# Tokens normalized inside the second graph layer, expert tiles gathered by an inverse list and scattered in token order

## What is computed

```python
x = x + gcn(_layernorm(x), edges, edge_weight)          # 2 graph layers, each segment_sum over 50000 edges
# _L0_ffn_ref on xt = _layernorm(x):
logits = xt @ Wr + br
probs = softmax(logits); top_p, top_idx = top_k(probs, 2)
weights = top_p / top_p.sum(-1)
xn = (xt - mu) * rsqrt(var + 1e-5)                      # a second normalization
xe = xn * ln_g[e] + ln_b[e]
h = gelu(xe @ W1[e] + b1[e]);  y = h @ W2[e] + b2[e]    # 8 experts, hidden size 1024
x = x + sum over the 2 chosen experts of weights * y
x = x + gru_gnn(_layernorm(x), edges, edge_weight)      # 5 rounds
x = x + ffn2(_layernorm(x))                             # 2 experts for all tokens
```

## Time and profile before

| | us |
|---|---|
| median of 3 runs | 4143.74 (4139.41 to 4147.3) |
| the profiled execution's own time | 4150.62 |
| its span, from first to last instruction | 4149.0 |
| PE busy | 3096.9 (75%) |
| DVE busy | 2347.8 (57%) |
| POOL busy | 1457.6 (35%) |
| ACT busy | 1234.0 (30%) |

### The profile page before, as it was taken

One profiled execution on the slowest core, in us unless ns is written; L12 is line 12 of the kernel. 1 busy time (PEld: TensorE's weight loads), 2 busy tenths in 40 slices (PEclk: granted clock), 3 DMA queues, 4 the chain that ended last, 5 costly groups with the idle time before them and its releaser, 6 DMA issues. The chain is left out here.

```text
span 4149.0 us, 55363 instructions
## 1 busy us (share of the span) xinstructions
PE 3096.9 (75%) x17934; PEld 2743.0 (66%) x17935; DVE 2347.8 (57%) x5512; ACT 1234.0 (30%) x2204; POOL 1457.6 (35%) x940
## 2 busy tenths in 40 slices
PE   2555541200799983199967999999999999999598
PEld 2544541100688872199866998998998898899465
DVE  7999991410587775066556555555545555545423
ACT  0000000110344431033323444444444444444122
POOL 1577777767777777676722000000000000000000
PEclk9999996655899995599988999999999999999699
DMA  9755543575666652654534343433333343432100
GB/s 399 261 140 121 141 110 74 127 213 124 165 172 168 184 138 6 208 121 99 129 103 162 123 133 119 133 123 122 131 124 121 126 137 111 130 122 89 46 21 21
DMA packets 378479, 549.06 MB, mean 132 GB/s; under 512 B 127283, under 2 KB 289114, under 8 KB 374234
## 3 DMA queue, kind: packets, MB, share of 16 engines
q1 hardware_dynamic: 242468, 464.88, 33.1%
q0 software_dynamic: 128400, 56.30, 10.9%
q10 hardware_dynamic: 7462, 25.89, 1.8%
HBM read 398.99 MB, written 147.99 MB: 132 GB/s over the span
## 5 line engine op out<-in xcount | busy, mean ns | idle before, releaser
L476 POOL DMA_INDIRECT plane_a<-pair,slot x392 | 653.5, 1667 | 379.9 <-issue 136.7
L476 POOL DMA_INDIRECT plane_w<-pair,slot x392 | 663.8, 1693 | 229.9 <-issue 122.7
L592 PE MATMUL bank<-ring_hi,h_hi 128*128 128x448 f32 x1750 | 652.8, 373 | 68.2 <-DVE ring_lo L1494 62.8
L1494 DVE TENSOR_TENSOR ring_lo<-ring_lo,ring_hi 128x448 fp32r<-128x448 f32 x875 | 523.4, 622 | 220.5 <-ACT ring_hi L1012 220.0
L592 PE MATMUL bank<-ring_lo,h_hi 128*128 128x448 f32 x1750 | 643.2, 368 | 0.0
L592 PE MATMUL bank<-ring_hi,h_lo 128*128 128x448 f32 x1750 | 643.0, 367 | 0.0
L1012 ACT ACTIVATE ring_hi<-ring_lo 128x448 fp32r<-128x448 f32 x875 | 499.0, 578 | 382.7 <-PE bank L592 376.7
L592 PE MATMUL bank<-gring_hi,hs_hi 128*128 128x512 f32 (+2 forms) x700 | 260.2, 372 | 293.0 <-DVE gring_lo L1266 293.0
L540 POOL DMA_DIRECT2D v_lo<-gru_v x5 | 3.6, 725 | 1320.7 <-PE bank L592 1307.1
L592 PEld LDWEIGHTS bank<-ring_hi,h_hi 128*128 128x128 f32 x1750 | 331.3, 189 | 97.0 <-issue 49.5
L565 PE MATMUL bank<-parts,eq 128*128 (+1 forms) x3136 | 133.0, 170 | 318.2 <-DVE hit_hi L1213 317.5
(11 more groups left out here) (301 smaller groups left out, 5923.7 us busy)
## 6 DMA issues: line engine op xcount, KB each, us to landing
ring_lo<-plane_w SPq DMA_DIRECT2D x175, 1120.0 KB, 5.4
gring_lo<-plane_a SPq DMA_DIRECT2D x50, 1280.0 KB
plane_a<-nat SPq DMA_DIRECT2D x25, 1600.0 KB, 45.1
plane_w<-nat SPq DMA_DIRECT2D x100, 400.0 KB
w_hl<-w_split POOLq DMA_DIRECT2D x16, 2048.0 KB
keyrow<-key_rows ACTq DMA_DIRECT2D x49, 512.0 KB
part_in<-in_L_ffn_W SPq DMA_DIRECT2D x16, 1024.0 KB
w_split<-part_hi SPq DMA_DIRECT2D x16, 1024.0 KB, 4.4
```

Of the source, the lines that this page charges most:

```text
L476: g_.indirect_dma_start(out=plane, out_offset=bass.IndirectOffsetOnAxis(slot[:, t:t + 1], 0), in_=pair[:, k, t:t + 1], in_offset=None, com ...
L592: last = mm(ps, lhs[x], rhs[y], start=start and n == 0, stop=stop and n == 2)
L1494: V.tensor_tensor(ring_lo[:, t, :], ring_lo[:, t, :].bitcast(FP32), ring_hi[:, t % HS, :].bitcast(FP32), ALU.subtract).then_inc(lo_rdy, 1)
```

## The change

1. The zero fill of `slots_x` is gone, and so is `slots_x`.
2. Inside the second graph layer, two chunks behind, DVE adds `x` to the finished tiles and takes their moments (`add_input`), ACT normalizes them (`normal_tokens`), PE transposes (`turn_chunk`) and forms logits (`logits`), DVE takes these (`take_logits`), and ACT makes the twice normalized tokens from one pair of factors and stores them to `tokens` in HBM (`keep_tokens`). The second normalization has no pass of its own. For 20 of the 25 tiles this lies inside the layer; chunks 12 and 13 (3 and 2 tiles) come after it. `x` is loaded at the start of the second layer.
3. From the slots, DVE makes one-hot matrices in bf16 (`in_lo`, `named`), and 50 matrix products on PE turn them into the inverse list: for each slot the token that it holds (`idx_x`) and the row of `chosen` where its result goes (`idx_y`).
4. POOL gathers each expert tile from `tokens` by an indirect DMA (`gather_tokens`) and scatters each result to `chosen` by another (`scatter_result`). Between them it issues the late `plane_w` scatters, now 21 batches, 2 or 3 scatters for each tile (`scatter_late`); `W1` is 28.
5. SP loads the weights of the experts, and after the experts loads `chosen` with plain DMAs of two rows for each token.
6. The last `layernorm(nat_b, res_b)` is written out (`straight_layernorm`). The first one, at the start, stays a loop.

```diff
-W1 = 31
+W1 = 28
...
+TN, TT, TG = 2, 12, 16
...
-    slots_x = nc.dram_tensor("slots_x", [ST * 128, D], FP32).ap()
-    slots_y = nc.dram_tensor("slots_y", [ST * 128, D], FP32).ap()
+    tokens = nc.dram_tensor("tokens", [NT * 128, D], FP32).ap()
+    chosen = nc.dram_tensor("chosen", [(ST + 2 * NT) * 128, D], FP32).ap()
...
-            for t in range(0, ST, 12):
-                n = min(12, ST - t)
-                sp.dma_start(slots_x[t * 128:(t + n) * 128, :].rearrange("(p c) f -> p (c f)", p=128), zeros[:, 0:n * D]).then_inc(xs_zeroed, 16)
...
+                if q == GCH:
+                    sp.wait_ge(used, NT * GCH)
+                    sp.dma_start(nat[:, 0:NT - 1, :], x_tiles).then_inc(x_in, 16)
+                    sp.dma_start(nat[0:LAST, NT - 1, :], a["x"][(NT - 1) * 128:N, :]).then_inc(x_in, 16)
...
+            sp.wait_ge(tok_kept, 16 * GCH)
+            load_expert(0)
+            load_expert(1)
+            sp.wait_ge(slots_ready, 1)
+            load_expert(2)
+            for e in range(3, X0):
...
+            by_tile = chosen[ST * 128:(ST + 2 * NT) * 128, :].rearrange("(k t p) f -> p k t f", k=2, p=128)
+
+            def load_chosen(t):
+                if t >= 4:
+                    sp.wait_ge(y_free, t - 3)
+                sp.dma_start(yg[t % 4], by_tile[:, :, t, :]).then_inc(y_got[t % 4], 16)
...
+                for t in range(r * RB, (r + 1) * RB):
+                    load_chosen(t)
+                if r + 1 < RR:
+                    load_panel_w(0, 0, r + 1)
...
-            for k in range(2):
-                for t in range(NT):
-                    g_.indirect_dma_start(out=slots_x, out_offset=bass.IndirectOffsetOnAxis(slot_u[:, k, t:t + 1], 0),
-                                          in_=nat2[:, t, :], in_offset=None).then_inc(x_sorted, 16)
-            pool.wait_ge(x_sorted, 16 * 2 * NT)
...
-                for k in range(2):
-                    g_.indirect_dma_start(out=yg[t % 4][:, k, :], out_offset=None, in_=slots_y,
-                                          in_offset=bass.IndirectOffsetOnAxis(slot_u[:, k, t:t + 1], 0)).then_inc(y_got[t % 4], 16)
...
+            def gather_tokens(i):
+                if i >= 3:
+                    pool.wait_ge(x_turned, i - 2)
+                g_.indirect_dma_start(out=xtile[:, i % 3, :], out_offset=None, in_=tokens,
+                                      in_offset=bass.IndirectOffsetOnAxis(idx_x[:, i:i + 1], 0)).then_inc(xt_in[i % 3], 16)
+
+            def scatter_result(i):
+                pool.wait_ge(y_rdy, i + 2)
+                g_.indirect_dma_start(out=chosen, out_offset=bass.IndirectOffsetOnAxis(idx_y[:, i:i + 1], 0),
+                                      in_=ytile[:, i % 2, :], in_offset=None).then_inc(y_out[i % 2], 16)
+
+            def scatter_late(n):
+                if n % G == 0:
+                    pool.wait_ge(scat_w, 16 * n)
+                g_.indirect_dma_start(out=plane_w, out_offset=bass.IndirectOffsetOnAxis(slot[:, n:n + 1], 0),
+                                      in_=pair[:, 0, n:n + 1], in_offset=None, compute_op=ALU.add).then_inc(scat_w, 16)
+
+            pool.wait_ge(tok_kept, 16 * GCH)
+            pool.wait_ge(idx_ready, 1)
+            for i in range(4):
+                gather_tokens(i)
+            for i in range(ST):
+                if i + 4 < ST:
+                    gather_tokens(i + 4)
+                if i >= 2:
+                    scatter_result(i - 2)
+                for n in range(G * W1 + G * (NB - W1) * i // ST, G * W1 + G * (NB - W1) * (i + 1) // ST):
+                    scatter_late(n)
+            scatter_result(ST - 2)
+            scatter_result(ST - 1)
...
+            def turn_chunk(q):
+                t0, tiles = GOFF[q - GCH] // 128, GWID[q - GCH] // 128
+                pe.wait_ge(conv_taken, min(q + 2, 2 * GCH))
+                pe.wait_ge(lg_taken, q - GCH)
+                pe.wait_ge(tok_ready, q - GCH + 1)
+                for j in range(tiles):
+                    for k in range(KD):
+                        last = tr(gate_ps[j][:, k * 128:(k + 1) * 128], nat[:, t0 + j, k * 128:(k + 1) * 128], ident[:, :])
+                    last.then_inc(tr_done, 1)
+
+            def logits(q):
+                t0, tiles = GOFF[q - GCH] // 128, GWID[q - GCH] // 128
+                pe.wait_ge(tr_out, t0 + tiles)
+                for j in range(tiles):
+                    for k in range(KD):
+                        last = mm(gate_ps[0][:, j * X0:(j + 1) * X0], xT[:, k, (t0 + j) * 128:(t0 + j + 1) * 128], ewr[:, k, :], start=(k == 0), stop=(k == KD - 1))
+                last.then_inc(lg_ps, 1)
...
+                    if t == TT and q >= GCH + 2:
+                        turn_chunk(q - 2)
+                    if t == TG and q >= GCH + 2:
+                        logits(q - 2)
...
+            for k in range(2):
+                pe.wait_ge(hits_ready, k + 1)
+                for t in range(k * NT, (k + 1) * NT):
+                    last = mm(bank[5][:, 0:2 * ST], in_lo[:, t, :], named[:, t, :, :].rearrange("p m n -> p (m n)"), start=(t == 0), stop=(t == 2 * NT - 1))
+            last.then_inc(idx_ps, 1)
...
+            def normal_tokens(q):
+                t0, tiles = GOFF[q - GCH] // 128, GWID[q - GCH] // 128
+                act.wait_ge(lroot, q - GCH + 1)
+                for t in range(t0, t0 + tiles):
+                    last = A(nat[:, t, :], res[:, t, :], ACT.Identity, bias=off2[:, 0, t:t + 1], scale=rstd2[:, 0, t:t + 1])
+                last.then_inc(tok_ready, 1)
+
+            def keep_tokens(q):
+                t0, tiles = GOFF[q - GCH] // 128, GWID[q - GCH] // 128
+                for j in range(tiles):
+                    t = t0 + j
+                    act.wait_ge(tr_done, t + 1)
+                    A(xT[:, :, t * 128:(t + 1) * 128], gate_ps[j][:, 0:D].rearrange("p (k n) -> p k n", k=KD), ACT.Copy).then_inc(tr_out, 1)
+                    evicted[0] += 1
+                for t in range(t0, t0 + tiles):
+                    last = A(nat[:, t, :], res[:, t, :], ACT.Identity, bias=off2[:, 1, t:t + 1], scale=rstd2[:, 1, t:t + 1])
+                last.then_inc(tok_scaled, 1)
+                act.wait_ge(tok_scaled, q - GCH + 1)
+                act.dma_start(tokens[t0 * 128:(t0 + tiles) * 128, :].rearrange("(t p) f -> p t f", p=128), nat[:, t0:t0 + tiles, :]).then_inc(tok_kept, 16)
...
+                    if t == TN and q >= GCH + 2:
+                        normal_tokens(q - 2)
...
+                    if t == TT + 1 and q >= GCH + 2:
+                        keep_tokens(q - 2)
+                    if t == MID + 18 and q > GCH:
+                        token_roots(q - 1)
...
+            def straight_layernorm(dst, src):
+
+                for t in range(NT):
+                    last = V.bn_stats(stats[:, t, :], src[:, t, :])
+                link(last)
+                moments(NT).then_inc(var_ready, 1)
+                inverse_root()
+                for t in range(NT):
+                    last = V.tensor_scalar(dst[:, t, :], src[:, t, :], mean[:, t:t + 1], rstd[:, t:t + 1], ALU.subtract, ALU.mult)
...
+            def add_input(q):
+                t0, tiles = tiles_of(q)[1:]
+                v.wait_ge(x_in, 64)
+                whole = min(tiles, NT - 1 - t0)
+                last = V.tensor_tensor(res[:, t0:t0 + whole, :], res[:, t0:t0 + whole, :], nat[:, t0:t0 + whole, :], ALU.add)
+                if whole < tiles:
                     link(last)
+                    last = V.tensor_tensor(res[0:LAST, NT - 1, :], res[0:LAST, NT - 1, :], nat[0:LAST, NT - 1, :], ALU.add)
+                link(last)
+                for t in range(t0, t0 + tiles):
+                    last = V.bn_stats(stats[:, t, :], res[:, t, :])
+                link(last)
+                at = slice(t0, t0 + tiles)
+                link(moments(tiles, t0, eps=0.0))
+                V.tensor_scalar(var2[:, 0, at], var[:, at], EPS, None, ALU.add)
+                V.tensor_scalar(var2[:, 1, at], var[:, at], 1.0 + EPS, EPS * EPS, ALU.mult, ALU.add).then_inc(lvar, 1)
...
+                        if t == MID + 15 and q > GCH:
+                            add_input(q - 1)
+                        if t == MID + 19 and q > GCH:
+                            token_scales(q - 1)
+                        if t == TG + 1 and q >= GCH + 2:
+                            take_logits(q - 2)
...
+            spread_over = lambda x, n: x.rearrange("p (t a) -> p t a", a=1).to_broadcast([128, NT, n])
+            for k in range(2):
+                at = slice(k * NT, (k + 1) * NT)
+                go(V.tensor_tensor(in_lo[:, at, :], row[:, :].rearrange("p (a n) -> p a n", a=1).to_broadcast([128, NT, 128]), spread_over(lo_f[:, at], 128), ALU.is_equal))
+                link(V.tensor_tensor(hit_of, row[:, 0:ST].rearrange("p (a n) -> p a n", a=1).to_broadcast([128, NT, ST]), spread_over(hi_f[:, at], ST), ALU.is_equal))
```

(16 more changed lines are left out.)

211 lines of the change are left out of this document (99 added, 112 removed).

## The result

The changed kernel took 4078.69 us (median of 4 runs, 4077.75 to 4081.05), the kernel before 4141.57 beside it (4 runs): a ratio of 0.9851, 95% interval 0.9832 to 0.9869. I had forecast 4050 with a range of 4012 to 4100. In the profiled executions the own time went from 4150.6 to 4078.94, 71.7 less, where the sum of my terms was 93.4. The direction and the mechanism came out, the size did not.

A forecast was written before the change was run, and what follows sets the result against it. PE bounded the experts before, at 7.1 us a tile; POOL was to pace them afterwards. Terms of -14.5, +13.0, -66.7, -17.4 and -7.8 sum to -93.4, taking the median from 4143.7 to 4050 us, range 4012 to 4100.

The forecast's parts named there:

- Rival 1: Expert loop: PE still bounds it, tiles take about 410 us instead of 485, total 3975; chance 7%.
- Term 1: POOL's second plane_a batch: without the zero fill only an ordinary landing wait remains, -14.5 us.
- everything after moves by it: Graph layers onward: POOL's 49 batches release the layers' panels, so all that follows comes 14.5 us earlier.
- Term 2: Second graph layer: PE's added transposes and logits for 20 tiles lengthen it, +13 us.
- bound of +6: Second graph layer: most that the load of x, queued ahead of a panel, was allowed to cost; costed at nothing.
- rival 3: Second graph layer: added DVE and ACT work is not hidden and PE's reserve empties, 31 us more, 4081; chance 11%.
- Term 3: End of graph layers to end of experts: list 55.2 plus POOL-paced loop 485 us, against 606.9, so -66.7.
- lower bound of 455: Expert loop: POOL's gathers, scatters and late plane_w scatters take 455 us if no landing wait is exposed.
- Term 4: Combination after the experts: earlier first combination (-4.1) and no DVE waits for gathers (13.3 saved), -17.4 us.
- Term 5: Last normalization: its two loops written out take 8.65 and 8.5 us instead of 12.24 and 12.83, -7.8.
- Rival 4: Expert loop: PE's clock falls to half, tiles take 809 us instead of 485, total 4374, slower; chance 5%.
- row of 200 to 640: Profile row, PE busy 228.66 of 440 us at full clock despite waits; grounds for forecasting full clock in the expert loop.

The follow-up runs named there:

- aligned run: Changed kernel with the same 168 late scatters dealt out so that each of the 21 late batches begins at a tile: 4043.77 us.
- version with three batches: Changed kernel with late batches begun at tiles, one plane_w scatter behind each of plane_a's batches 26 to 48, W1 = 32: 3976.59 us, 0.9627 of the kernel before.
- written-out version: Kernel before with only the two loops of the last normalization written out: 4128.85 us against 4138.03, ratio 0.9975.
- both covered ones with the panel first: Changed kernel, batches begun at tiles, plane_w scatters between plane_a's last batches, ring panel loaded before results: 3995.15 us with two batches there, 3976.59 with three.

## Why the prediction was right, and where its sum was wrong

- **The bound.** I had POOL as the pace of the new expert loop, at 8.0 us a tile before waits, and PE with waits in each. That holds: the loop without late scatters is 403.8, with them 503.9, and POOL's own times add up to it. It took 8.8 us a tile where I had 8.5. Rival 1 (PE still bounds, 3975) falls.
- **Term 1** was -14.5 and the trace of the pair says -15.1, but that agreement is partly luck. The second batch moved by 13.9 as forecast. The layers moved by 9, and the profile of before was a late one. The step that failed is "everything after moves by it". It also explains part of why medians differ by 63 where the two profiled executions differ by 71.7: before's profiled time of 4150.6 lies above all of its other runs.
- **Term 2** was +13.0 and is +17.4. The price of transpositions and logits is right (13.9). Put at nothing were the load of x (1.9) and a wait behind ACT's list, which came once, ahead of the last projection, and let the clock fall in it (1.1); the bound of +6 and rival 3 had named both kinds.
- **Term 3** was -66.7 and is -47.1. The list was right to 0.7 us. The loop's step that failed is the landing waits: I let a third of the batches stand right behind a gather and a scatter and charged 1.7 for each other one. That share was right (8 of 21 showed no wait), and nine bare batches waited 1.7 to 1.8 as charged. The other four waited 17.9 together: 5.2 and 6.2 bare and 3.5 in spite of a gather and a scatter, all three while expert weights came in at 365 to 400 GB/s, and 3.0 at 21 GB/s, which I can't explain. So one price for every landing was the mistake. The aligned run shows what all 33.9 us of waits were worth, 30 us: by the order of POOL's list alone the loop comes to 473.6, 19 above my lower bound of 455 ("no wait exposed").
- **Term 4** was -17.4 and is -14.0. The waits inside the combination went. The first combination was to come after 5.5 us, "a landing of 2, then a panel and a tile"; it took 7.8 from the scatter's end, because the panel was issued in the same moment as that scatter and its landing waited for the panel. The rest of the term was 13.3 and is 12.2.
- **Term 5** was -7.8 and is -9.2 by its own stretch, -10.0 in the kernel before alone. The passes came as forecast; the waits between them shrank too, which I had not counted.
- **The clock.** Rival 4 had a chance of 5% and did not come, but the clock did fall: in ten pieces of 3 to 13.5 us of the loop the granted clock is 0.50. I had forecast 1.00 and named a fall there as a sign that the forecast is wrong; the sign came, without the cost. Stretches of the loop around the 6.2 us wait, columns as in the earlier trace rows:

```profile
1724.00:1732.00 8.00, 6.78 (x44) 6.03 (x44) 4.16 (x8) 2.45 (x4) 1.60 (x2) 1.00 0.83 252
1732.00:1736.00 4.00, 0.00 (x0) 0.00 (x0) 0.00 (x0) 0.00 (x0) 3.39 (x3) 0.75 1.05 400
1736.00:1742.00 6.00, 1.01 (x3) 0.62 (x4) 0.82 (x3) 0.00 (x0) 4.80 (x4) 0.50 0.81 251
1742.00:1748.00 6.00, 6.00 (x19) 4.75 (x19) 1.46 (x5) 0.42 (x1) 5.06 (x4) 0.53 0.27 44
```

PE was idle from 1731 to 1740, the granted clock went to 0.50, the 1.2 GHz level, at 1734, and was back at 1.00, the 2.4 GHz level, by 1748. Over the loop it was 0.93, and PE's busy time 415.8 where it is 388.5 without late scatters. By the row of 200 to 640 I had kept the full clock, and that was wrong. The Trainium skill, TensorE: Matmul & The Clock Gate, section HAM oscillation, which I had set against it, describes a fall behind the wait in each round; here it came nine times in 57 tiles after the start, five of them behind a wait of PE of 2.4 to 8.4 us. After the loop's start it cost nothing, since POOL then waited for nothing but landings and went on issuing. In the version with three batches PE is nearly the pace, and there the clock is 0.97.

## What to carry to other kernels

When work moves to an engine that issues many small transfers, add up that engine's busy time, its issue gaps and its waits for landings separately, and ask of each wait what stands right ahead of it: here the same 168 scatters cost 30 us more or less by where their batches began. A landing takes longer beside a large load, so count the batches that end in one. A wait for a landing is room for a transfer into another tensor: 24 scatters put there cost nothing. The layers also started 18 us earlier, since POOL met fewer long pauses; the filled waits do not explain that, so it is not a gain to count on elsewhere. When a large gain comes out smaller, cut both traces at the same events first, and look at one more run of the kernel before: its profiled run may itself be early or late by 5 us in one stretch.

## What the runs showed of the hardware

- **A round of the GRU has two lengths.** The period of a chunk is 44.99 us in most rounds and 45.88 in some, always for a whole round, with PE busy throughout. Of 13 profiled executions seven have it in the first round (the changed kernel's among them), before in the last, its written-out version in the fourth; four have none (aligned, both covered ones with the panel first, and the one without late scatters). Products took 368 ns in the last round where it was long, and 365 in the last rounds of the others. It makes up to 5 us between runs, so two kernels are better compared by stretches than by own time. I have not found its cause.
- **POOL's scatter takes long beside a long instruction of DVE, and not beside large loads.** A plane_w scatter takes 1.54 us of POOL. In the kernel before one took 7.02 with almost no DMA traffic, while DVE added x in one instruction of 6.56 us (1547.04):

```profile
1548.00 7.02 POOL L476 DMA_INDIRECT plane_w<-pair,slot  x1 [0.30 <-issue]
1548.00:1555.00 7.00, 0.00 (x0) 0.00 (x0) 6.59 (x4) 0.00 (x0) 7.00 (x1) 0.50 0.14 4
```

In the changed kernel's loop 21 scatters stood beside more than 250 GB/s and took 1.58 us on average, the others 1.57. That DVE is the cause is read from traces only; no run moved a DVE instruction to test it.
- **A landing takes longer beside large loads.** Behind a gather and a scatter (2.6 us) no batch waited where DMA moved less than 185 GB/s, and 20 waited 2.4 to 3.5 us at 235 to 389.
- **A small scatter's landing waits for a large load that is issued with it:** from the last scatter's start to the next load's issue 5.8 to 6.1 us with a panel of 1.1 MB issued in the same moment, 2.6 without. In the run without late scatters the panel was issued 1.6 us ahead of the scatter, and it was 4.1.
